# Two state-space layers run as one program of 64 chunks, each image's group norm formed inside the loop

## The reference

```python
xz = seq @ W_in.T                      # 64 -> 2 x 128
u, z = jnp.split(xz, 2, axis=-1)
u = silu(causal_conv_4_taps(u) + conv_b)
x_dbl = u @ W_x.T                      # dt (4), B (16), C (16)
dt = softplus(x_dbl[..., :4] @ W_dt.T + b_dt)
h = exp(dt * A) * h + (dt * u) * B_t   # per step, 128 channels x 16 states
y = sum_s(h * C_t) + u * Dp
out = (y * silu(z)) @ W_out.T
```

## Time and profile before

| what | value |
| --- | --- |
| median of 3 runs | 6244.23 us (6240.84 to 6248.35) |
| the profiled execution | 6251.4 us, its span 6249.6 us |
| first scan of layer 1 / of layer 2 | at 114.0 us / at 2031.1 us of the span |
| last addition to X in layer 2 of the four | ends at 3850.9 us |
| mean granted TensorE clock | 0.93 of full |

### The profile page before, as it was taken

The page is one execution under the profiler, slowest core; times in us unless marked ns, Lnnn a source line. Parts: engine busy times, 40 slices in busy tenths (PEclk is TensorE's granted clock), DMA queues, the critical chain, the costliest instruction groups (busy, mean ns, idle before and its releaser), DMA issues. The chain is left out here.

```text
span 6249.6 us, 78158 instructions
## 1 busy us (share of the span) xinstructions
PE 5093.4 (81%) x22462; PEld 2637.8 (42%) x22462; DVE 4940.1 (79%) x6854; ACT 3285.8 (53%) x3643; POOL 4764.7 (76%) x2174
## 2 busy tenths in 40 slices
PE   3888888888884888888888887881548989989897
PEld 1333333333332343333433344520225656656565
DVE  5999999999995999999999997105457676776665
ACT  3555555555552555555555553000436767767776
POOL 3999999999993999999999996000236767767675
PEclk9999999999996999999999998795779999999999
DMA  3555555555552555555555553491348999999999
GB/s 129 202 197 199 205 201 197 201 203 205 199 197 81 196 205 197 201 201 206 200 201 199 205 199 126 171 402 32 79 102 161 188 168 188 181 172 188 186 188 207
DMA packets 1423977, 1150.93 MB, mean 184 GB/s; under 512 B 1216728, under 2 KB 1226096, under 8 KB 1415792
## 3 DMA queue, kind: packets, MB, share of 16 engines
q1 hardware_dynamic: 1423858, 1149.56, 64.9%
HBM read 814.23 MB, written 21.09 MB: 134 GB/s over the span
## 5 line engine op out<-in xcount | busy, mean ns | idle before, releaser
L633 POOL TENSOR_TENSOR l_state<-l_state,l_c_row 128x1024 f32<-128x1024 f32 x1024 | 2405.0, 2367 | 73.9 <-DVE l_state L593 69.4
L469 PE MATMUL l_y_ps<-l_state,ident 128*128 128x512 f32 x4096 | 1992.3, 613 | 47.4 <-POOL l_state L633 46.8
L1495 POOL TENSOR_TENSOR l3s_el<-l3s_s_sb,l3s_eh 128x1024 f16<-128x1024 f32 (+2 forms) x584 | 1168.7, 2012 | 1129.0 <-ACT l3s_s_sb L1480 1117.0
L593 DVE TENSOR_TENSOR_SCAN l_state<-l_decay,l_b_ps 128x1024 f32<-128x1024 f32 x704 | 1608.9, 2285 | 73.4
L469 PEld LDWEIGHTS l_y_ps<-l_state,ident 128*128 128x128 f32 x4096 | 784.8, 196 | 869.8 <-issue 679.6
L1503 DVE TENSOR_SCALAR_CACHE_REDUCE l3s_s_sb<-l3s_s_ps 128x512 f32<-128x512 f32 (+1 forms) x1096 | 753.2, 689 | 490.2 <-PE l3s_s_ps L1439 468.2
L1452 PE MATMUL l3s_o_ps<-l3s_vt,l3s_et 128*128 128x257 f16 x4368 | 878.5, 279 | 204.6 <-DMA l3s_et<-l3s_el 143.6
L1479 ACT ACTIVATE l3s_eh<-l3s_s_sb,l3s_shift 128x1024 f16<-128x1024 f32 (+2 forms) x584 | 634.6, 1087 | 548.0 <-DMA l3s_et<-l3s_el 448.3
L579 DVE TENSOR_TENSOR l_b_ps<-l_dtu,l_b_ps 128x1024 f32<-128x1024 f32 x704 | 850.4, 1208 | 31.2 <-PE l_b_ps L457 29.4
L457 PE MATMUL l_b_ps<-l_bc,mamba_pick 128*128 128x512 f32 x1408 | 575.6, 491 | 292.0 <-DVE l_state L593 282.4
L1454 PE MATMUL l3s_o_ps<-l3s_vt,l3s_et 128*128 128x129 f16 x4368 | 787.9, 224 | 0.0
(11 more groups left out here) (356 smaller groups left out, 5439.9 us busy)
## 6 DMA issues: line engine op xcount, KB each, us to landing
l_c_row<-l_c_rows SPq DMA_DIRECT2D x1024, 512.0 KB, 3.8
l_b_row<-l_c_rows SPq DMA_DIRECT2D x320, 512.0 KB, 5.0
l_ring_a<-in_L_conv_W SPq DMA_DIRECT2D x28, 1024.0 KB, 10.9
l2b_ring_b<-in_L_conv_W SPq DMA_DIRECT2D x26, 1024.0 KB, 10.9
l_xs<-X SPq DMA_DIRECT2D x64, 256.0 KB, 5.4
l_ring_a<-in_L_conv_W SPq DMA_DIRECT2D x14, 704.0 KB, 12.7
l2b_ring_b<-in_L_conv_W SPq DMA_DIRECT2D x13, 704.0 KB, 12.7
l_ring_a<-in_L_conv_W SPq DMA_DIRECT2D x14, 640.0 KB, 12.1
```

The lines of the kernel that those rows point to most:

```text
L469: last = nc.tensor.matmul(y_ps[:, half(h)], C["ident"][:, :], state[:, s % STATES, half(h)], start=False, stop=(s == S - 1))
L593: nc.vector.tensor_tensor_scan(state[:, s % STATES, :], by, add, 0.0, ALU.mult, ALU.add).then_inc(s_scan, 1)
L633: nc.gpsimd.tensor_tensor(state[:, s % STATES, :], state[:, s % STATES, :], c_row[:, s % C_ROWS, :], ALU.mult).then_inc(s_hc, 1)
L1495: nc.gpsimd.tensor_tensor(el[:, part, off:off + EXPW], s_sb[:, par, j * EXPW:(j + 1) * EXPW], eh[:, part, off:off + EXPW], ALU.subtract).t ...
```

## The change

Both layers become one program of 64 chunks (`mamba_layers`), written out for every engine without a loop. `prepare` takes the place of the constants, the weights and the first norm: SP sends for the four images, ACT's queue for the 18 weight arrays of both layers, and only image 0 is waited for and normed (32 `bn_stats`). The statistics of image 1 are taken on DVE while chunk 0 is prepared. All later norms are formed by `ImageNorm` inside the loop: those of the images 2 and 3 (two `bn_stats` behind the scan of the units 3, 7, 11 and 15 of chunks 0 to 7), the four images of layer 2 and the images 0 and 1 for layer 3 (one `bn_stats` at each of these units, from chunk 8's unit 15 to chunk 56). The small steps of an image's norm are spread over four chunks, one to a unit; its sums over the partitions are products of PE into the second half of `prep_ps` at unit 14, read by DVE at unit 15. The root is formed by Ln and Exp, so ACT keeps one table. Layer 3 norms the images 2 and 3 alone. The write of the C rows moves from SP's slot 11 to 8, ahead of the load of `xs`, and its source `c_out` now shares its memory with `gu`.

```diff
@@ GroupNorm.vector (layer 3 calls it with first=2)
-                for b in range(B):
+                for b in range(self.first, B):
@@ prepare, on DVE
+                for i in range(2):
+                    scale_taps(i)
+                dve.wait_ge(s_x[0], 16)
+                for g in range(G):
+                    norm.stat(0, g)
+                norm.step(dve, 0, 0)
+                copy_turned(0)
...
+                copy_turned(1)
+                norm.read(dve, sum_ps[1], 0, 1)
...
+                norm.row(dve, 0, 1)
+                norm.read(dve, sum_ps[0], 0, 2)
@@ constants of the loop
-LOAD_AT, C_WRITE_AT = 8, 11
+LOAD_AT, C_WRITE_AT = 8, 8
+TOTAL = 2 * CHUNKS
+STAT_UNITS = (3, 7, 11, 15)
+STEP_AT = ({1: 0, 3: 1, 5: 2}, {1: 3, 3: 4, 5: 5}, {8: 6, 9: 7, 11: 8, 12: 9, 14: 10}, {})
+ROOT_AT, SUMS = {5: 0, 6: 1}, {0: 0, 1: 1, 3: 2}
+ROW_AT, SUM_AT, READ_AT = {1: 0, 3: 1}, 14, 15
@@ ImageNorm
+    def stat(self, j, g):
+        image = j % B
+        self.nc.vector.bn_stats(out=self.stats[:, j % 2, g * 6:(g + 1) * 6],
+                                in_=self.Xv[:, image, :, 2 * g:2 * g + 2]).then_inc(self.s_stats, 1)
@@ pe_prep, act_prep
                     wait(pe, s_xt, n + 1)
+                    wait(pe, norm.s_read, norm_reads_before(n - 1))
...
-                nc.scalar.activation(xt[:, :], prep_ps[:, 0:HALF], ACT.Identity, scale=scale_c[:, bass.ds(n, 1)],
+                act.wait_ge(norm.s_read, norm.reads(image + 1))
+                nc.scalar.activation(xt[:, :], prep_ps[:, 0:HALF], ACT.Identity, scale=norm.norm_c[:, image, 0:1],
...
-                wait(act, s_cw, 16 * n)
+                wait(act, s_u, n + 1)
                 nc.scalar.activation(c_out[C_AT:C_AT + BLOCK, :], prep_ps[C_AT:C_AT + BLOCK, :],
...
-                wait(act, s_u, n + 1)
+                wait(act, s_cw, 16 * (n + 1))
                 nc.scalar.activation(gu[:, :], prep_ps[:, :], ACT.Identity, bias=1.0).then_inc(s_one, 1)
@@ units
+            if s == SUM_AT:
+                pe_norm(pe, c)
...
+            act_norm(act, c, s)
...
                 dve_prep(dve, c + 1, 1 - par, s)
+            dve_norm(dve, c, s)
             if s == ADD_AT and not is_first(c):
                 dve_add(dve, c - 1)
             dve_scan(dve, c, par, s)
+            dve_stats(dve, c, s)
@@ run
-            for c in range(FIRST):
-                chunk(c, c % 2)
-            with eng.Fori(0, (LAST - FIRST) // 2) as i:
-                chunk(2 * i + FIRST, FIRST % 2)
-                chunk(2 * i + FIRST + 1, 1 - FIRST % 2)
-            chunk(LAST, LAST % 2, False)
+            for c in range(TOTAL):
+                for s in range(S):
+                    unit_step(eng, c, c % 2, s, c < LAST)
```

More of the change, by code:

```diff
@@ L222, in _ @@
[L222 to L236, removed]
@@ new lines, in _ @@
+                nc.vector.memset(C["one"][:, :], 1.0).then_inc(s_one, 1)
+                dve.wait_ge(s_done, 1)
+                for i in range(2):
+                    scale_taps(i)
[4 more added lines that the diff above has]
+                copy_turned(0)
+                norm.step(dve, 0, 1)
+                norm.step(dve, 0, 2)
+                norm.read(dve, sum_ps[0], 0, 0)
+                for i in range(3, 6):
+                    norm.step(dve, 0, i)
@@ L241, in _ @@
+                copy_turned(1)
+                norm.read(dve, sum_ps[1], 0, 1)
+                dve.wait_ge(s_done, 3)
+                for i, unit in enumerate(DVE_UNITS):
+                    nc.vector.tensor_copy(C["pick"][:, i * P:(i + 1) * P], pick[:, unit * P:(unit + 1) * P])
+                for i in range(6, NORM_STEPS):
+                    norm.step(dve, 0, i)
+                norm.row(dve, 0, 0)
+                norm.row(dve, 0, 1)
+                norm.read(dve, sum_ps[0], 0, 2)
             @block.tensor
@@ L636, in is_first, with norm_reads_before, pe_norm, act_norm @@
         def is_first(c):
-            return isinstance(c, int) and c == 0
+            return c == 0
+        def norm_reads_before(c):
+            return sum(1 for k in SUM_OF if k < c) + 3
+        def pe_norm(pe, c):
+            if c in SUM_OF:
+                wait(pe, s_sz, c + 2)
+                norm.sum(pe, spare_ps, *SUM_OF[c])
+        def act_norm(act, c, s):
+            j, phase = NORM_JOB.get(c, (None, None))
+            if phase == 2 and s in ROOT_AT:
+                norm.inverse_root(act, j, ROOT_AT[s])
+        def dve_stats(dve, c, s):
+            j, groups = stats_at(c, s)
+            for g in groups:
+                if g == 0:
+                    if j < B:
+                        dve.wait_ge(s_x[j], 16)
+                    else:
+                        dve.wait_ge(s_add, PER_IMAGE * (j - B + 1))
+                norm.stat(j, g)
+        def dve_norm(dve, c, s):
+            if c not in NORM_JOB:
+                return
+            j, phase = NORM_JOB[c]
+            if s in STEP_AT[phase]:
+                norm.step(dve, j, STEP_AT[phase][s])
+            if phase == 3 and j < 2 * B and s in ROW_AT:
+                norm.row(dve, j, ROW_AT[s])
+            if s == READ_AT and c in SUM_OF:
+                norm.read(dve, spare_ps, *SUM_OF[c])
         def behind(c, par, s, lag):
```

475 lines of the change are left out of this document (295 added, 180 removed).

## The result

The changed kernel takes 6274.16 us (median of 5 runs, 6269.25 to 6282.32), the kernel before beside it 6242.15 (5 runs, 6232.59 to 6248.35). The ratio is 1.0051, 95% interval 1.0038 to 1.0064: slower by 0.5%, where 6162 and "faster" were forecast. The gap between the layers went and the start became shorter, both near what was worked out. The loop took back more than both gave.

A forecast was written before the change was run, and what follows sets the result against it. DVE was taken to set the loop's pace, with about 0.7 us of waits a chunk. From 6251.4, -99.6 (seam), -31.5 (start), -1 (layer 3) and +50 (loop) gave 6169.3, as a median 6162 us; range 6120 to 6215.

The forecast's parts named there:

- The small steps: Nine norms in the loop, 198 small DVE instructions, mostly in the gap between drive and scan: 8 us, bounds nothing and 30.
- The seam: Between the two state-space layers: drain, weights, norm of all images and cold first chunk all go, -99.6 us.
- The start: Before chunk 0: weights land at 22, norm ready at 42 instead of 73.5, -31.5 us, bounds -22.5 and -40.5.
- The statistics: 256 statistics on DVE in the loop at 0.194 us, all on the path: 49.7 us, upper price 71.9.
- Given back: Statistics at units 11 and 15 fill the gate's wait, not unit 11's: about 8 us, bounds 0 and 43.
- Layer 3's norm: Layer 3's shorter norm, given 1 us for the narrower chain: -1.
- Each added instruction costs more: Rival: 0.28 us a statistic and 0.15 a step in the loop, nothing given back: 6214 us; 17 in 100.
- my case: The prediction's main case: median 6162 us, faster, own range 6140 to 6185; 62 in 100.
- The program starves: Rival: engines wait for instruction fetch of the written-out 64 chunks, 2 us a chunk: 6286 us, slower; 5 in 100.
- The waits swallow more: Rival: added DVE work fills the whole 0.7 us of waits a chunk, 43 us instead of 8: 6127; 13 in 100.
- it doesn't do what it says: Rival: a norm comes too late, chunk 32 waits as before, the 99.6 us stay: 6262, slower; 2 in 100.
- The signs named beforehand: Trace signs: gates 57.4 to 57.6 apart with four statistics, POOL's idle about 1.7 us a chunk; wrong if gates above 58.

The follow-up runs named there:

- no_steps: The changed kernel without the small steps of the norms inside the loop, the statistics kept; 6172.43 us, ratio to the kernel before 0.9882.
- before_written_out: The kernel before with the 32 chunks of each layer written out, without the hardware loop; 6247.65 us, ratio to the kernel before 1.0007.

## Why the prediction was wrong, by its own steps

- **The small steps**: this step failed. It priced 198 instructions at 8 us, since "a step of about 0.1 fits in" the 0.23 us between a drive and its scan. They cost 101.7 by removal: most of those that work within SBUF stand until a POOL instruction ends, and no gap of 0.23 us holds that. (The terms named add up to 0.74 a norm and not 0.85, which changes nothing.) The trace of before had no DVE instruction in the loop that works on SBUF alone: each drive, scan and gate there reads or writes PSUM, and so do its other lines in that window. So the nearest rows were of another kind, and the bound above (0.15 each, 30 us) was taken from them as well. Priced by the start of the changed kernel, where POOL rests, the steps still look like 0.19. Where they do read PSUM they cost 2 us, and the forecast of 8 would have stood. The Trainium skill ("SBUF — State Buffer", SBUF: two separate sides) states the rule: a VectorE operation in a 2-port perf mode and a GpSimd operation take turns at one pair of ports, and so do one with two SBUF inputs and a GpSimd operation that reads SBUF; whoever comes second stands until the other's whole instruction is over. The runs agree, with 1.41 us against 0.19, and with the same wait for the copy from SBUF to SBUF. The rule speaks against this change. A forecast by it could have been worked out from rows that were there: POOL is 98% busy with instructions of 2.36 us, so some 1.2 us a step. For the 173 steps and copies within SBUF that makes 208 us, twice the 101.7 (43 of them were short), but slower and not faster.
- **The seam**, -99.6: there is no gap around chunk 32; its norm was there in time. The term can't be measured apart from the loop's pace, so with the gap gone it holds by its definition, and all that is over is put to the loop.
- **The start**, -31.5: the first scan came 27.9 earlier. The weights were in at 27.5 and not at 22; from there to the norm it took 17.8 and not 20. The 13 that the prediction drew from the Trainium skill's rule of the queues didn't come. The rule itself isn't refuted: 431 packets of each queue moved from 5 to 20 us, as taking turns gives. But a turn let through 14.6 KB of X and 0.2 KB of weights, so the weights still trailed X. Besides, ACT's own issue was held for 13.1 us; what held it no run shows. Of the 27.9 only 21.9 reach the first gate, since chunk 0 holds small steps; in no_steps that gate is 5.7 us earlier.
- **The statistics**, +49.7: 57.2 by removal, 0.22 each for 0.194. The next instruction starts 0.19 after a statistic, as forecast, so the other 9 us aren't in the statistics themselves, and I didn't follow them. In the kernel before the same number costs 23. There they stand between a drive and its scan, where 0.23 us are empty; in the changed kernel they stand behind a scan, where nothing is. That the place makes the difference was not tried by itself.
- **Given back**, -8: the gate's wait did go, but the wait at unit 11 rose, by 11.6 us in 1700 in no_steps, since more chunks met it. Its clock of 0.50 was on the list as a reason why it doesn't fill; that it grows was not.
- **Layer 3's norm**, -1: the first product behind it stands 1.4 us nearer to chunk 62's gate. The other 9.7 us between that gate and the end are no gain of the change: before_written_out, whose layers 3 and 4 are those of the kernel before, needs 2444.5 us for this stretch where the profiled execution of the kernel before needs 2456.2 and the changed kernel 2445.1. So it is the profiled execution of the kernel before that took longer there.
- **The rivals**. "Each added instruction costs more" erred the same way as my case, only less: it had 0.28 a statistic and 0.15 a step, for every short instruction alike. "The program starves" had the number nearest to the result, 6286, and that is luck: before_written_out refutes it. "The waits swallow more" and "it doesn't do what it says" didn't happen.
- **The signs named beforehand** pointed the right way: gates above 58 were to show it wrong, and most stand at 59 to 66 where there are steps. POOL's idle before its product went to 4 us a chunk, not 1.7.

With 101.7 in place of 8 the sum of the prediction is 6256. The 18 us left to 6274 are the start (4), the statistics (7) and what wasn't given back (8), as far as costs by removal can be added.

## What to carry to other kernels

Before an instruction goes into a queue as filler, look at where its operands lie and what the other engines run at that time, not at its size: on VectorE beside a busy GpSimd, a small product of two SBUF tensors or a copy within SBUF lasted until GpSimd's running instruction ended, or the next one. Look for a form of the step that reads PSUM, or put it in GpSimd's own queue. And when the trace has no instruction of the added kind under the same neighbours, the upper bound is a neighbour's whole duration (2.4 us here), not that of the nearest row.

## What the runs showed of the hardware that was not expected

- A copy of 128x32 from SBUF to SBUF waits as long as a product of two SBUF tensors (1416 and 1413 ns); a statistic over 128x128 in SBUF doesn't (293 ns).
- Of 256 such products, 55 ended not with POOL's running instruction but with the one behind it, after 2.4 us.
- POOL's instructions stay at 2.36 us beside the waiting steps; what it loses is the wait for the next scan.
- An ACT queue with weight DMAs stood 13.1 us in one issue, beside four loads of X on SP's queue. Both queues moved 431 packets in 15 us, X 6.28 MB and the weights 0.08.
- Written out for all chunks, the program ran at the pace of the loop of two (1.0007).
